# Two gated linear attentions: their entry laid beside the first tiles, and the output gate projected per tile

## The reference, cut to what matters

```python
x = x + _L0_ffn_ref(_layernorm(x, axis=-1), Wq, Wk, Wv, ...)
...
q1 = (x @ Wq) * scale;  k1 = x @ Wk;  v = x @ Wv          # 8 heads of 64
q2 = (x @ Wqa @ Wqb) * scale
k2 = softmax((x @ Wka @ Wkb).reshape(B, L, H, DK), axis=-1)
gk1 = log_sigmoid(x @ Wg1a @ Wg1b + bg1) / 16             # gk2 likewise
e = softmax(x @ We); rw = e * one_hot(argmax(e))           # 4 experts, one is chosen
o_dense  = chunk_gla(q1, k1, v, gk1)
o_sparse = sum over experts of chunk_gla(q2 * rw, k2 * rw, v, gk2 * mask)
g = x @ Wga @ Wgb
o = (o_dense + o_sparse) * rsqrt(mean(o * o) + EPS) * norm_w
o = o * (g * sigmoid(g))                                   # the output gate
return o.reshape(B, L, H * DV) @ Wo
```

## Time and profile before

| | |
|---|---|
| median of 3 runs | 3475.22 us (3474.63 to 3477.32) |
| the profiled execution | 3475.21 us, span 3474.0 us |
| mean granted clock of TensorE | 0.897 |
| PE busy | 3070.3 us, 88% |
| DVE busy | 2655.0 us, 76% |
| ACT busy | 1994.2 us, 57% |
| POOL busy | 945.2 us, 27% |
| DMA | 35.38 MB, mean 10 GB/s |
| first GLA, first bn_stats to first scores | 675.67 to 772.50 us |
| second GLA, first bn_stats to first scores | 1797.80 to 1895.36 us |

### The profile page before, as it was taken

How to read it: one execution, slowest core, us unless ns; L and a number is a source line. 1 busy time by engine, 2 the same in 40 slices (tenths; PEclk the granted TensorE clock), 3 DMA queues, 4 the chain that set the end, 5 groups by cost and what they waited for, 6 DMA issues and landing times. The chain is left out here.

```text
span 3474.0 us, 58769 instructions
## 1 busy us (share of the span) xinstructions
PE 3070.3 (88%) x23668; PEld 1418.3 (41%) x23668; DVE 2655.0 (76%) x3291; ACT 1994.2 (57%) x3671; POOL 945.2 (27%) x973
## 2 busy tenths in 40 slices
PE   6999999889999699999989999856666877999879
PEld 2222222246666222222224666512223543666745
DVE  8999999636666899999963666679896555887544
ACT  4999999635554499999954555443332235444022
POOL 0000000123333000000012333346674520676400
PEclk7999999869999699999986999968797987999779
DMA  2000000000000100000000000000000000000000
GB/s 90 13 16 15 14 15 15 8 0 1 2 2 2 55 15 15 15 15 15 15 11 1 1 2 1 24 0 0 0 0 9 1 0 0 1 1 1 1 1 13
DMA packets 30218, 35.38 MB, mean 10 GB/s; under 512 B 13623, under 2 KB 24058, under 8 KB 29690
## 3 DMA queue, kind: packets, MB, share of 16 engines
q1 hardware_dynamic: 29754, 31.56, 3.1%
q10 hardware_dynamic: 192, 0.07, 0.0%
HBM read 19.15 MB, written 7.34 MB: 8 GB/s over the span
## 5 line engine op out<-in xcount | busy, mean ns | idle before, releaser
L387 DVE TENSOR_REDUCE max_parts<-banks 128x2 f32<-128x1024 f32 x1024 | 1169.1, 1217 | 18.9 <-PE banks L275 18.8
L477 ACT ACTIVATE probs<-banks 128x512 f32<-128x512 f32 x2048 | 1082.4, 599 | 74.0 <-PE banks L282 56.9
L275 PE MATMUL banks<-k_parts,q_parts 48*128 48x512 bf16 x2048 | 621.5, 396 | 48.4 <-DMA k_parts<-k_scratch 24.2
L282 PE MATMUL banks<-q_parts,k_parts 51*128 51x512 bf16 x2048 | 655.1, 386 | 6.6
L300 PE MATMUL banks<-probs,v_heads 128*9 128x256 f32 x8192 | 637.8, 383 | 7.5 <-ACT pv_copy L488 0.2
L282 PEld LDWEIGHTS banks<-q_parts,k_parts 51*128 51x128 bf16 x2048 | 148.0, 94 | 482.8 <-ACT probs L477 418.0
L517 POOL CAST neg_max_parts<-neg_max 128x8 bf16<-128x8 f32 x64 | 12.9, 201 | 1151.5 <-DVE neg_max L392 1151.5
L300 PEld LDWEIGHTS banks<-probs,v_heads 128*9 128x9 f32 x8192 | 123.7, 88 | 379.2 <-issue 340.5
L1315 PE MATMUL banks<-decay,ident 128*128 128x512 f32 x256 | 155.8, 756 | 106.1 <-POOL decay L1281 106.1
L1281 POOL TENSOR_TENSOR decay<-state,c_row 128x1024 f32<-128x1024 f32 x64 | 212.2, 3337 | 78.8 <-DVE state L1344 78.8
L1344 DVE TENSOR_TENSOR_SCAN state<-decay,state_carry,state 128x1024 f32<-128x1024 f32 x64 | 209.6, 3313 | 0.0
(11 more groups left out here) (432 smaller groups left out, 5375.6 us busy)
## 6 DMA issues: line engine op xcount, KB each, us to landing
outT_half<-pv_copy SPq DMA_DIRECT2D x252, 16.0 KB
prob_sums<-pv_copy SPq DMA_DIRECT2D x252, 2.0 KB
q_scratch<-qk_parts SPq DMA_DIRECT2D x8, 384.0 KB, 3.9
k_scratch<-qk_parts SPq DMA_DIRECT2D x8, 384.0 KB, 2.5
k_parts<-k_scratch SPq DMA_DIRECT2D x32, 96.0 KB
q_parts<-q_scratch SPq DMA_DIRECT2D x28, 96.0 KB
k_parts<-k_scratch SPq DMA_DIRECT2D x32, 64.0 KB
q_parts<-neg_max_rows SPq DMA_DIRECT2D x128, 3.0 KB
```

The lines of the kernel that those rows point to most:

```text
L275: nc.tensor.matmul(Mb[m % 2][:, blk(x)], Q[p % 2][half_of(x, ROWS), tile(t)], K[p % 2][half_of(x, ROWS), blk(b)], start=True, stop=True).t ...
L282: nc.tensor.matmul(bank("exp", n, x)[:, :], K[p % 2][half_of(x, ROWS + PARTS), tile(t)], Q[p % 2][half_of(x, ROWS + PARTS), blk(j)], start ...
L387: nc.vector.tensor_reduce(mxp[s % 2][:, :, u // NB, u % NB], Mb[m % 2].rearrange("p (x k) -> p x k", x=2), AX.X, ALU.max).then_inc(*maxed. ...
L477: nc.scalar.activation(PT[:, n % RING, x, :], bank("exp", n, x)[:, :], ACT.Exp, scale=float(HD) ** -0.5).then_inc(*exped.inc())
```

## The change

`layer_norm_T` and `gla_front` no longer run ahead of a GLA; their work is issued by `gla_ffn` itself, block by block. PE's order ahead of the loop is now turn, low_gates, route and low_rank of block 0, then the first gates and values, then block 1 and so on, with tile 0's preparation between the blocks; four PSUM banks that the loop uses later (3 to 6) serve these entries in rotation. The layer norm's `apply` of blocks 1 to 3 is on POOL. The low-rank gate projections of a block are one matmul with 113 output rows in place of three, the weights having zero columns between; ACT copies them and adds the ones of the bias rows. Routing is done once for tiles 0 to 3 ahead of the loop, and once for tiles 4 to 15 within tile 0; the masks of blocks 1 to 3 are turned after tile 0's project, their products are made after tile 1's. The output gate is projected per tile in the loop (four matmuls of 128 columns into one bank, a new use `gp` in the rotation); its sigmoid is Exp, Ln, Exp on ACT; DVE multiplies gate, norm weight and sigmoid (`weigh_gate`). The table loads are gone, and so are the two meetings of all engines.

```diff
-TILE_USES = "cum0 cum1 v klow q2 half g0 g1 k1 q1 rs tk0 tq0 tk1 tq1 out".split()
+EARLY, MASKED = 4, 17
+FIRST_USES = "v klow q2 cum0 cum1 half g0 g1 gp k1 q1 tk0 tq0 tk1 tq1".split()
+TILE_USES = "cum0 cum1 v klow q2 half g0 g1 gp k1 q1 rs tk0 tq0 tk1 tq1 out".split()
+MASK_TURNS, SAME_EXPERTS = 0, 1
...
+            def low_gates(b):
+                pe.wait_ge(norm.copied, b + 1)
+                pe.wait_ge(*entry.before("glow", b))
+                nc.tensor.matmul(entry.bank("glow", b)[0:113, :], w["Wa"][:, 128:241], g.xnT[:, blk(b)], start=True, stop=True).then_inc(*gates_low.inc())
...
+            def gate_project(t):
+                pe.wait_ge(*bank_read("gp", t))
+                pe.wait_ge(gates_copied, t // 4 + 1)
+                for r in range(4):
+                    i = nc.tensor.matmul(bank("gp", t)[:, tile(r)], w["Wc"][0:64, tile(r)], a2T[0:64, tile(t)], start=True, stop=True)
+                i.then_inc(*gate_projected.inc())
...
+            pe.wait_ge(weights_in, 1)
+            turn(0); low_gates(0); route(0); low_rank(0); turn(1); gates(0); values(0)
+            low_gates(1); low_rank(1); route(1); turn_mask(entry, 0); low_keys(0); low_queries(0)
+            same_expert(entry, 0); cumulate(0); turn(2); low_gates(2); low_rank(2); route(2)
+            halves(0); gates(1); gate_project(0); keys(0); queries(0)
+            turn(3); low_gates(3); low_rank(3); route(3)
+            turn_k0(0); turn_q0(0); turn_k1(0); turn_q1(0)
+            for t in range(NT):
...
                 if t + 2 < NT:
                     gates(t + 2)
+                if after:
+                    gate_project(t + 1)
...
+                for b in range(1, NB):
+                    if t == MASK_TURNS:
+                        turn_mask(ring, b)
+                    if t == SAME_EXPERTS:
+                        same_expert(ring, b)
...
+            def weigh_gate(t):
+                dve.wait_ge(gate_sigmoid, t + 1)
+                dve.wait_ge(gated, t - 1)
+                nc.vector.scalar_tensor_tensor(flat(gate[t % 2]), bank("gp", t)[:, :], w["norm"], flat(sg), ALU.mult, ALU.mult).then_inc(*gate_made.inc())
...
                 if after:
                     decay_keys(t + 1)
                     dense_queries(t + 1)
+                    weigh_gate(t + 1)
+                add_state_dense(t)
+                if t == MASK_TURNS:
+                    choose_experts(1, others)
+                normalise(t)
+                add_x(t)
+                if t == SAME_EXPERTS:
+                    for b in range(1, NB):
+                        mask_same(ring, b)
...
+            def sigmoid(t):
+                act.wait_ge(gate_projected, t + 1)
+                act.wait_ge(gate_made, t)
+                nc.scalar.activation(flat(sg), bank("gp", t)[:, :], ACT.Exp, scale=-1.0).then_inc(*gate_exped.inc())
+                act.wait_ge(gate_exped, t + 1)
+                nc.scalar.activation(flat(sg), flat(sg), ACT.Ln, bias=1.0).then_inc(*gate_logged.inc())
+                act.wait_ge(gate_logged, t + 1)
+                nc.scalar.activation(flat(sg), flat(sg), ACT.Exp, scale=-1.0).then_inc(*gate_sigmoid.inc())
...
                 if t + 2 < NT:
                     softplus(t + 2)
+                if after:
+                    sigmoid(t + 1)
...
-    layer_norm_T(g)
-    g.rest(gla_in)
-    gla_ffn(g, views(ffn_w, GLA_COLS))
+    gla_ffn(g, views(ffn_w, GLA_COLS), gla_in)
```

More of the change, by code:

```diff
@@ L853, in project @@
                 i.then_inc(*projected.inc())
-            gates(0)
-            for t in range(-1, NT):
-                now, after = t >= 0, t + 1 < NT
-                if now:
-                    scores(t, 0)
+            pe.wait_ge(weights_in, 1)
+            turn(0)
+            low_gates(0)
+            route(0)
+            low_rank(0)
+            turn(1)
+            gates(0)
+            values(0)
+            low_gates(1)
+            low_rank(1)
+            route(1)
+            turn_mask(entry, 0)
+            low_keys(0)
+            low_queries(0)
+            same_expert(entry, 0)
+            cumulate(0)
+            turn(2)
+            low_gates(2)
+            low_rank(2)
+            route(2)
+            halves(0)
+            gates(1)
+            gate_project(0)
+            keys(0)
+            queries(0)
+            turn(3)
+            low_gates(3)
+            low_rank(3)
+            route(3)
+            turn_k0(0)
+            turn_q0(0)
+            turn_k1(0)
+            turn_q1(0)
+            for t in range(NT):
+                after = t + 1 < NT
+                scores(t, 0)
                 if after:
                     cumulate(t + 1)
-                if now:
-                    scores(t, 1)
-                    spread_experts(t)
+                scores(t, 1)
+                spread_experts(t)
                 if after:
@@ L981, in add_x @@
                 nc.vector.tensor_tensor(g.x_tok[:, t, :], g.x_tok[:, t, :], bank("out", t)[:, 0:128], ALU.add).then_inc(*x_added.inc())
[L983 to L990 removed]
+            first, others = slice(0, EARLY), slice(EARLY, NT)
+            norm.statistics(0)
+            norm.apply(0)
+            norm.statistics(1)
+            highest_logit(0, first)
+            norm.statistics(2)
+            choose_experts(0, first)
+            finish_gates(0)
+            subtract_max(0)
+            mask_same(entry, 0)
+            norm.statistics(3)
+            normalise_keys(0)
+            expert_queries(0)
+            finish_gates(1)
+            decay_keys(0)
+            dense_queries(0)
+            weigh_gate(0)
+            dve.wait_ge(zeroed, 2)
+            highest_logit(1, others)
+            for t in range(NT):
+                after = t + 1 < NT
+                state_decay(t)
+                mask_scores(t, 0)
+                mask_scores(t, 1)
+                mask_queries(t)
                 if after:
```

435 lines of the change are left out of this document (226 added, 209 removed).

## The result

| | before | after |
|---|---|---|
| median of 4 runs | 3474.93 us (3473.96 to 3477.32) | 3516.53 us (3515.16 to 3517.08) |
| span of the profiled execution | 3474.0 | 3515.8 |
| mean granted clock | 0.897 | 0.902 |
| a GLA, its first bn_stats to the next layer's | 451.1, 450.1 | 471.9, 472.5 |

Slower by 1.2%, clear of the spread of the runs: ratio 1.0118, interval 1.0101 to 1.0136. The forecast had 3491, range 3452 to 3533: side and range held, but the 41.6 us are more than twice the 16 forecast. All of it lies in the two GLAs (20.8 + 22.4 = 43.2 of their spans; elsewhere -1.4).

A forecast was written before the change was run, and what follows sets the result against it. The front was taken as long by order and clock, the loop as bound by TensorE. Terms -94.4 + 32.7 + 46.5 + 20.2 + 11 summed to +16, so 3491 us; the range leaving out two in ten was 3452 to 3533.

The forecast's parts named there:

- step 1: Ahead of each GLA's loop: new front of 50 us in place of 96.8 and 97.6, -94.4 us in all.
- 2 gate projection: In the loop on TensorE: eight instructions of 128 columns, 1.09 us per tile, +32.7 us over 30 tiles.
- Step 3: Ahead of sum_squares: TensorE waits 1.55 us per tile for the gate's PSUM bank, read by weigh_gate, +46.5 us.
- Step 4: In tiles 0 and 1: routing and masks of blocks 1 to 3 delay the loop 10.1 us per GLA, +20.2 us.
- step 5: In the loop: gate_project lengthens the small-matmul stretch, 24 clock falls of 1.6 us in place of 17, +11 us.
- Step 6: weigh_gate and sigmoid covered by air of DVE and ACT; POOL's mask rows and wider weight DMA also cost nothing.
- Rival B: In the loop: the bank wait is hidden, the sum without its 46.5 us, 3445 us; chance 0.08.
- Rival C: Between sum_squares and next scores: TensorE's standstill drops the clock a second time per tile, +48, 3539 us; chance 0.17.
- Rival A: The front wins: scores start at 45 us, falls stay 17, one-offs 7, sum -11, 3464 us; chance 0.2.
- Rival D: Ahead of the loop: the new front stays serial at 70 us, 3531 us; chance 0.07.

The follow-up runs named there:

- e3: Changed kernel with POOL's constants and zero state written behind its first apply instead of at the start: 3511.15 us, ratio 1.0106 to the kernel before.
- e8: As e3, with the layer norm's applies of blocks 1 to 3 on DVE in place of POOL: 3512.06 us, ratio 1.0107 to the kernel before.
- e1: Changed kernel with weigh_gate(t+1) moved in DVE's order from behind dense_queries to behind finish_gates(t+2): 3467.9 us, ratio 0.9983 to the kernel before.
- e6: Changed kernel with choose_experts(1) of tile 0 moved ahead of add_state_dense(0) in DVE's order: 3522.34 us, ratio 1.0132 to the kernel before.
- e4: Changed kernel without output gate (projection, sigmoid, weighing left out, different result), bank rotation of before: 3411.1 us, ratio 0.9823 to the kernel before.
- e11: Changed kernel with gate_project's four matmuls issued twice in tiles 1 to 15, result unchanged: 3582.18 us, ratio 1.0309 to the kernel before.
- e2: Changed kernel with gate_project moved from behind gates to behind update(t, 1), sigmoid behind square, bank wait kept: 3489.97 us, ratio 1.0046 to the kernel before.
- e5: Changed kernel with gate_project between the experts' inter and update, sigmoid behind square, weigh_gate ahead of decay_keys: 3462.19 us, ratio 0.996 to the kernel before.
- e9: As e2, but from tile 1 the gate is projected into the dense state's bank, rotation as before the change: 3464.51 us, ratio 0.9967.
- e12: As e10, with halves(t+1) moved behind spread_experts, bank rotation and ACT's order following: 3457.29 us, ratio 0.9954 to the kernel before.
- e7: Changed kernel with the edits of e5, e3 and e6 together: 3454.44 us, ratio 0.9937 to the kernel before.
- e10: Changed kernel with the edits of e9, e3 and e6 together: 3450.17 us, ratio 0.993 to the kernel before.

## Why the prediction was off

Both GLAs together, in microseconds; the measured terms are from the lengths of tiles and fronts in the two traces.

| term | forecast | measured |
|---|---|---|
| 1 new front | -94.4 | -84.0 |
| 2 gate projection | +32.7 | +32.7 |
| 3 bank wait | +46.5 | +50.7 (30 x 1.69) |
| rest of a tile without fall, 30 x 0.07 | 0 | +2.1 |
| 4 routing, with the falls of tiles 0 to 2 (2.2 of the forecast's 11) | +22.4 | +24.1 |
| 5 falls, tiles 3 to 14 (the other 8.8) | +8.8 | +17.5 |
| sum | +16 | +43.1 |

The mechanism was right in steps 2, 3, 4 and 6, and with them the side; 27 us are missing in the sizes, all with the same sign. The two terms that failed are step 1, the new front (50 us forecast, 54.9 and 55.5 measured, 10.4 in all), and step 5, the clock falls (8.8 forecast, 17.5 measured). Together they are 19 of the 27.

*Step 1, 50 us a front, was 55 (+10.4 in all).* The forecast walked the queues: copy_low_gates(0) over at T+8.0, finish_gates(0) at 14.8, cumulate at 22.5, the end of the second finish at 38.5. After has them so (instructions in order of time), with T = 676.44:

```profile
685.28 0.69 ACT L1214 ACTIVATE low_rank_gates<-banks,bias_rows 113x512 f32<-113x512 f32 x1 [2.14 <-PE banks L783]
...
694.84 1.29 DVE L1083 SCALAR_TENSOR_TENSOR log_decay<-banks,abs_logit 128x512 f32<-128x512 f32 x2 [3.57 <-ACT abs_logit L1245]
...
702.52 2.08 PE L841 MATMUL banks<-log_decay,cum 128*128 128x512 f32 x2 [1.38 <-DVE same_expert_tri L1072]
...
718.88 1.29 DVE L1083 SCALAR_TENSOR_TENSOR log_decay<-banks,abs_logit 128x512 f32<-128x512 f32 x2 [10.06 <-ACT abs_logit L1245]
...
731.38 1.16 PE L897 MATMUL banks<-q_decayedT,k_decayedT 64*128 64x128 f32 x16
```

that is T+9.5, 18.4, 26.1, 43.7 and, for the scores, 54.9. It is 1.5 late at the first copy, 3.6 at the first finish, 5.2 at the end of the second. The first part is POOL's constants beside apply(0), to which the forecast gave no cost: in e3 (T = 675.54) the copy is over at T+8.1. The second part stays in e3, with finish_gates(0) at T+16.9: softplus(0) starts at T+13.6, and ACT stands idle before it for 1.36 us, released by gates(0) on TensorE (L826 in e3's rows). The walk had gates(0) over at 12. They come late since TensorE does that whole stretch at 1.2 GHz. The front's middle figure of 50 lay between bounds of 47, "mostly at 2.4 GHz", and 53; a mean granted clock of 0.62 means 42 of 55 us at 1.2 GHz. The e3 fronts of 50.8 and 51.9 meet the 50 partly by errors that cancel: the second finish is still 3 late there, and the last stretch 2.2 shorter than forecast. What sets a front's clock is open; POOL's constants account for 2.2 us of each front and no more.

The moved applies were priced at most 2.8 us per block, from a row of POOL with another shape (128x512, 0.69); they took 3.13 to 3.41, and e8 shows that this cost nothing.

*Step 3 misses by 4.* The place, the releaser and the order were right (e1 takes it all back). Row by row, queries to dense_queries, its slot and weigh_gate made 2.41 in the forecast and 2.55 in the trace. Rival B (the wait is hidden) is out; only e1's edit made it true.

*Step 4 was right:* tile 0 is longer by 5.95 us in each GLA (6 forecast), and TensorE waits 3.07 for choose_experts ahead of normalise(0). In e6 this wait is gone and the program is no faster.

*Step 5 is the one with a wrong picture.* I counted falls as something that a tile has or has not, 24 in place of 17, and set the top bound at one in each of 30. The runs show lengths: the low stretch can be 6.8 us in one piece, 3.2 us of loss. In tiles 3 to 14 there are 24 units against 13. e4 (6 per GLA without gate_project), after (12) and e11 (mean 1.9 a tile with twice of it) tie them to gate_project being in the tile. e2 (3 per GLA) shows that its place matters while the bank wait is there; e5 and e9 (13 each, gate_project elsewhere) show that it does not once the wait is gone. The forecast's reason, a longer stretch of small matmuls beside the gates, is thus not shown. That it leaned to more falls was right, and how many was a guess. Rival C's 3539 is nearer to the result than my 3491, but by luck: it placed its falls at the standstill, where the clock of after stays at 1.00, and e1 has the falls without the standstill.

*Step 6, nothing for DVE and ACT,* was right: without the wait (e1) the shortest tile is 22.55, which is 21.48 + 1.07, so TensorE sets it.

Rival A, the front wins, is what e4 comes to: without any gate the kernel is 63.8 us below before. The gate in the loop took all of that and 41.6 more; 51 of these 105 went for a bank. Rival D (a serial front of 70 us) is out by the 55.

Open: how much of the falls is the length of the small-matmul stretch, and how much the way in which the length of a tile meets the clock. Against the first alone stand e5 and e9 (gate_project apart, falls in every tile); against the second alone e2 against after (tiles of the same 24.33, 3 and 12 falls). Nor is it shown why two long falls come in tile 2 of e6, why e12 has one of 13.6 us, and what sets the clock of a front, which lasts from 50.0 (e11) to 55.5 us (after) with the same instructions.

## What to carry to other kernels

A use put into a rotation of PSUM banks moves every later use to another bank: go down the new list and ask for each who reads the bank it now gets, and what that reader stands behind in its queue; here one new entry cost 51 us and one moved call on DVE gave them back. When TensorE is the bound and its work is a written order of small matmuls, price an added group at more than its duration, for it also changes what the clock does. Here 1.07 us more per tile cost 1.8 with the bank wait cured, wherever the group stood, and the second dose beside the gates (e11) cost twice its duration. Look at every tile's length after each edit, since the falls come and go with it; two local gains (e6, e12) were lost that way. Where work is laid on an idle engine, look at what the others do at that moment: POOL's constants beside DVE's first apply cost 2.2 us a front (e3), while the applies moved to POOL cost nothing (e8).

## What the runs showed of the hardware that I had not expected

- Four 128x128 float32 tensor_scalar of DVE: 1.11 us alone, 3.31 us while POOL wrote constants (memsets and affine selects). One of POOL's affine selects (128x64) took 1.09 us there, and 0.23 in e3, where DVE was not doing its applies.
- A clock fall can be twice as long, 6.8 us at 1.2 GHz in one piece with TensorE busy throughout, and costs 3.2 us; in e12 one lasts 13.6 us, and its tile is 5.7 us longer.
- The same front of a GLA, with the same instructions, lasts 54.2 us at a mean clock of 0.62 and 51.8 at 0.66 in the two GLAs of e7.
- The kernels without a wait settle at one fall in nearly each tile, 24.11 to 24.23 us long (e1, e5, e9, e10), whether the gate is projected at one place or another; before, at 21.5 us, only about every other tile had one. With 0.9 us of fall in the mean tile before (17 x 1.6 over 30) and 1.6 now, the 1.07 us of new work cost 1.07 + 0.7 per tile.
- TensorE had the same busy time in 250 us of after and of e2 (234.66 us) at mean clocks of 0.93 and 0.98: busy time says nothing of the clock.
